# Moving every second q copy from VectorE to ScalarE, and re-ordering GpSimd's norms and first row gathers, in a spiking-attention and expert kernel

## What is computed

```python
Q, K, V = (lif(layer_norm(xn @ W.T + b), 1.0) for W, b in ...)       # spikes: 0 or 1
attn = Dh - (q_sum + k_sum - 2.0 * qk) + log_pe_bias(N, N)            # no softmax, so linear
out = lif(einsum(attn * scale, V), 0.5)
s = lif(layer_norm(out @ Wo.T + bo), 1.0)                             # output spikes
...
ids = argmin(dist2(rms_norm(xn), centroids))                          # one of 8 experts a row
y = einsum(a * silu(g), down_w[e])                                    # a, g = rms_norm(xn) @ up_w[e]
out = y + xn                                                          # of the row's own expert
```

## Time and profile before

| what | value |
|---|---|
| time, median of 3 runs | 383.24 us |
| lowest and highest | 380.7 and 385.92 us |
| the profiled execution's own time | 383.15 us |
| its span, from the first to the last instruction | 381.4 us |
| mean granted clock of PE | 0.991 of full speed |

### The profile page before, as it was taken

One profiled execution on the slowest core, in us unless ns is written; L12 is line 12 of the kernel. 1 busy time (PEld: TensorE's weight loads), 2 busy tenths in 40 slices (PEclk: granted clock), 3 DMA queues, 4 the chain that ended last, 5 costly groups with the idle time before them and its releaser, 6 DMA issues.

```text
span 381.4 us, 9230 instructions
## 1 busy us (share of the span) xinstructions
PE 359.4 (94%) x2455; PEld 302.9 (79%) x2464; DVE 310.2 (81%) x798; ACT 237.4 (62%) x631; POOL 239.4 (63%) x311
## 2 busy tenths in 40 slices
PE   8989999999998999997889999999999999999992
PEld 4768788877886888886778888888888888888881
DVE  5969999999978788998757777788877777788884
ACT  4477788878864768793535555555565555555561
POOL 4868577786760249986656666666666666666643
PEclk9999999999999999999989999999999999999998
DMA  7585668654359921565122222223223232232000
GB/s 222 185 273 183 162 195 227 225 146 140 111 129 218 238 83 57 167 188 152 51 84 79 66 71 87 69 80 96 77 81 84 79 89 76 90 95 63 29 16 0
DMA packets 31921, 45.42 MB, mean 119 GB/s; under 512 B 4161, under 2 KB 25858, under 8 KB 31764
## 3 DMA queue, kind: packets, MB, share of 16 engines
q1 hardware_dynamic: 25248, 29.73, 26.9%
q0 software_dynamic: 6416, 15.26, 14.0%
q10 hardware_dynamic: 228, 0.10, 0.1%
HBM read 36.84 MB, written 15.63 MB: 138 GB/s over the span
## 4 chain that ended last, share of the span: by engine, by line
PE 41%; DVE 27%; DMA 13%; issue 8%; ACT 5%; POOL 5%; DVEq 0%; ACTq 0%; POOLq 0%
PE bank L698 12%; PE bank L717 10%; DMA row_a<-rows_a,slot_id 9%; PE bank L501 3%; PE bank L615 3%; PE bank L576 3%; ACT d_hi L926 3%; DVE v_sp L1128 2%; DVE q_sp L1128 2%; DVE k_sp L1128 2%; PE bank L670 2%; PE bank L681 2%; DVE st L995 2%; DVE q_t L1139 2%; DMA thr<-lim_rows 2%
## 5 line engine op out<-in xcount | busy, mean ns | idle before, releaser
L1369 DVE TENSOR_TENSOR d_lo<-down_sb,d_hi 128x1024 fp32r<-128x1024 f32 x38 | 46.6, 1227 | 31.2 <-ACT d_hi L926 31.0
L1514 POOL DMA_INDIRECT row_a<-rows_a,slot_id x39 | 41.2, 1056 | 43.8 <-DVE e_o L1351 42.2
L926 ACT ACTIVATE d_hi<-down_sb 128x1024 fp32r x38 | 40.3, 1060 | 45.1 <-PE bank L717 35.4
L1562 POOL DMA_INDIRECT out_x<-e_o,slot_id x39 | 45.6, 1168 | 19.4 <-issue 14.1
L698 PE MATMUL bank<-up_hi,e_xh 128*128 x156 | 52.4, 417 | 0.0
L1520 POOL DMA_INDIRECT row_s<-rows_s,slot_id x39 | 39.1, 1002 | 15.9 <-issue 11.3
L698 PE MATMUL bank<-up_hi,e_xl 128*128 x156 | 48.5, 392 | 0.4 <-DVE e_xl L1310 0.4
L698 PE MATMUL bank<-up_lo,e_xh 128*128 x156 | 48.4, 392 | 0.0
L897 ACT ACTIVATE e_xh<-bank 128x256 fp32r<-128x256 f32 x39 | 15.0, 386 | 40.4 <-PE bank L670 40.4
L824 ACT ACTIVATE junk<-bank 128x256 bf16<-128x256 f32 x96 | 35.5, 380 | 6.7 <-PE bank L501 6.6
L501 PE MATMUL bank<-w_hi,x_hi 128*128 128x264 f32 (+1 forms) x128 | 35.6, 359 | 0.7 <-DVE dots L1132 0.7
(11 more groups left out here) (241 smaller groups left out, 981.3 us busy)
## 6 DMA issues: line engine op xcount, KB each, us to landing
up_raw<-in_up_w SPq DMA_DIRECT2D x16, 512.0 KB, 3.9
rows_a<-xn SPq DMA_DIRECT2D x32, 129.0 KB, 2.3
rows_a<-in_x SPq DMA_DIRECT2D x8, 512.0 KB, 11.8
xs<-in_x SPq DMA_DIRECT2D x7, 512.0 KB, 4.1
down_sb<-in_down_w SPq DMA_DIRECT2D x5, 512.0 KB, 6.1
rows_s<-s_out SPq DMA_DIRECT2D x8, 256.0 KB, 3.2
down_sb<-in_down_w SPq DMA_DIRECT2D x6, 256.0 KB, 3.1
blk_tab<-in_blocks SPq DMA_DIRECT2D x1, 1024.0 KB, 5.4
```

The costliest lines, as they stand in the source:

```text
L926: act.activation(d_hi[:, :, :], down_sb[:, bass.ds(e, 1), :, :].rearrange("p a c n -> p (a c) n"), ACT.Copy).then_inc(d_high, 1)
L1369: V.tensor_tensor(d_lo[:, :, :], down_sb[:, bass.ds(e, 1), :, :].rearrange("p a c n -> p (a c) n"), (d_hi if k < ST else d_end)[:, :, :].b ...
L1514: G.indirect_dma_start(row_a[s % 4][:, :], None, rows_a, bass.IndirectOffsetOnAxis(ap=slot_id[:, s:s + 1], axis=0), bounds_check=N - 1, oo ...
L1562: G.indirect_dma_start(out, bass.IndirectOffsetOnAxis(ap=slot_id[:, s:s + 1], axis=0), e_o[s % 4][:, :], None, bounds_check=N - 1, oob_is_ ...
```

## The change

Four things are changed.

1. In the projection stage the copy of the turned q tile of every odd tile but the last (tiles 1, 3, ..., 29: fifteen copies) is made by ACT, at the end of its step, instead of by DVE.
2. `norms_out` works on a whole chunk of four tiles: one addition and one power over four values a partition, where there were two of each over two values. It waits for all four squares, and DVE for all four factors.
3. POOL's first gathers stand in another order: after the norms of chunks 6 and 7 no gather is issued; `gather_a(2)` and `gather_a(3)` follow both; `gather_a(4)` comes after the first two `gather_s` instead of after the fourth.
4. In the last round of the attention ACT makes the squares of chunk 6 ahead of the last high part of the weights instead of behind it.

```diff
+        def kept_by_act(t):
+            return t % 2 == 1 and t < NT - 1
...
@@ (ACT, at the end of step_a)
+                if k >= 3 and kept_by_act(k - 3):
+
+                    act.wait_ge(qt_done, t - 2)
+                    act.activation(q_home(t - 3), qt_bank[:, 0:P].bitcast(BF16).rearrange("p (c n) -> p c n", c=DC),
+                                   ACT.Copy).then_inc(qt_kept, 1)
...
@@ (ACT, the attention's rounds)
                 attention_spikes(c)
+                squares_out((c - 1) % 2, (c - 1) // 2)
                 if c == NCH - 1:
                     high_parts(E - 1, (1,))
-                squares_out((c - 1) % 2, (c - 1) // 2)
...
@@ (DVE, at the end of step_a, and in output_spikes)
-                if 0 <= k - 3 < NT:
+                if 0 <= k - 3 < NT and not kept_by_act(k - 3):
                     keep_qt(k - 3, 0)
...
-                    dve.wait_ge(wo_rs, 2 * c + pair + 1)
+                    dve.wait_ge(wo_rs, c + 1)
...
@@ (POOL)
-                for pair in range(2):
-                    of = lambda buffer: buffer[:, bass.ds(c * CH + 2 * pair, 2), 3:4].rearrange("p a b -> p (a b)")
-                    held(wo_sq, CH * c + 2 * pair + 2)
...
+                of = lambda buffer: buffer[:, bass.ds(c * CH, CH), 3:4].rearrange("p a b -> p (a b)")
+                held(wo_sq, CH * (c + 1))
+                held(wo_rs, c - 1)
+                G.tensor_tensor(pv[:, k, :], of(ss), eps4[:, :], ALU.add).then_inc(out_n, 1)
+                held(out_n, c + 1)
+                G.tensor_tensor(of(rs), pv[:, k, :], half_neg[:, :, 0], ALU.pow).then_inc(wo_rs, 1)
...
-                if c >= 4 and c < NCH:
+                if c in (4, 5):
                     gather_a(c - 4)
+            gather_a(2)
+            gather_a(3)
             for k in range(2):
                 pool.wait_ge(s_put[k], 16 * NCH // 2)
-            for k in range(4):
-                gather_s(k)
+            gather_s(0)
+            gather_s(1)
+            gather_a(4)
+            gather_s(2)
+            gather_s(3)
...
             for s in range(4, ST):
-                gather_a(s)
+                if s > 4:
+                    gather_a(s)
                 gather_s(s)
                 scatter(s - 4)
```

More of the change, by code:

```diff
@@ L166, in build @@
         b16, _ = place("b16", [P, 24], BF16)
-        eps3, _ = place("eps3", [P, 3], F32)
+        eps4, _ = place("eps4", [P, CH], F32)
         half_neg, _ = place("half_neg", [P, 4, 2], F32)
@@ L307, in after, with q_home @@
                 eng.wait_ge(s, count)
+        def kept_by_act(t):
+            return t % 2 == 1 and t < NT - 1
+        def q_home(t):
+            c, at = t // CH, t % CH * P
+            return q_t[c // 2][:, c % 2, :, at:at + P]
         def x_tile(t):
@@ L1136, in keep_qt @@
                 dve.wait_ge(qt_done, t + 1)
-                at = k % CH * P
-                c = t // CH
-                V.tensor_copy(q_t[c // 2][:, c % 2, :, at:at + P],
+                V.tensor_copy(q_home(t),
                               qt_bank[:, 0:P].bitcast(BF16).rearrange("p (c n) -> p c n", c=DC)).then_inc(qt_kept, 1)
@@ L1402, in held @@
                 pool.sem_inc(pool_passed, 1)
-            G.memset(eps3[:, :], D * LN_EPS)
+            G.memset(eps4[:, :], D * LN_EPS)
             step(G.memset(half_neg[:, :, :], -0.5))
@@ L1434, in norms @@
                 held(rs_done, t - 1)
-                G.tensor_tensor(pv[:, s, 0:3], tile_of(ss, t)[:, 0:3], eps3[:, :], ALU.add).then_inc(norm_n, 1)
+                G.tensor_tensor(pv[:, s, 0:3], tile_of(ss, t)[:, 0:3], eps4[:, 0:3], ALU.add).then_inc(norm_n, 1)
                 held(norm_n, t + 1)
@@ L1501, in norms_out @@
                 c = k + 2 * i
-                for pair in range(2):
-                    of = lambda buffer: buffer[:, bass.ds(c * CH + 2 * pair, 2), 3:4].rearrange("p a b -> p (a b)")
-                    held(wo_sq, CH * c + 2 * pair + 2)
-                    held(wo_rs, 2 * c + pair - 1)
-                    G.tensor_tensor(pv[:, pair, 0:2], of(ss), eps3[:, 0:2], ALU.add).then_inc(out_n, 1)
-                    held(out_n, 2 * c + pair + 1)
-                    G.tensor_tensor(of(rs), pv[:, pair, 0:2], half_neg[:, 0, :], ALU.pow).then_inc(wo_rs, 1)
+                of = lambda buffer: buffer[:, bass.ds(c * CH, CH), 3:4].rearrange("p a b -> p (a b)")
[4 more added lines that the diff above has]
+                G.tensor_tensor(of(rs), pv[:, k, :], half_neg[:, :, 0], ALU.pow).then_inc(wo_rs, 1)
             def gather_a(s):
```

## The result

| | median us (range, runs) | ratio to before | 95% interval |
|---|---|---|---|
| the changed kernel | 380.62 (379.37 to 382.05, 15) | 0.9938 | 0.9911 to 0.9965 |
| the kernel before, beside it | 382.47 (380.70 to 386.02, 15) | 1 | |

The change makes the kernel 0.6% faster, where I had forecast 1.5%: 2.4 us by the ratio, 1.9 by the medians, against 5.7. The time lies inside the range (374.2 to 381.3), the gain is less than half of what I forecast. Two sizes have to be explained: what came, and what went away again.

A forecast was written before the change was run, and what follows sets the result against it. DVE's list was taken to bound the projections, then PE, with waits for rows in the expert steps. 383.15 - 3.6 (copies) - 2.0 (gathers, including the norms' 0.8) gave 377.5 us; range 374.2 to 381.3.

The forecast's parts named there:

- Part 1: Projections: eleven copies at 0.33 us leave DVE's chain, gaining 3.6 us, with PE late next.
- the bound of 5.0: Projections: upper limit of the copies' gain, all fifteen counting at 0.33 us, 5.0 us.
- rivals b and c: Projections: ACT becomes the bound; copies give nothing, 381.2 us, chance 0.10, or kernel slower than before, 387.2 us, chance 0.04.
- Part 2: Output norms before the experts: spikes end and first gather of spikes goes out 0.8 us earlier, bounds 0 and 1.0.
- the start of the spikes at 182.3: POOL's first gather of spikes, issued at 182.3 instead of 183.11 thanks to earlier norms.
- Part 3: First expert steps: reordered gathers start tile 5 at 197.0 instead of 198.97, gaining 2.0 us, bounds 1.1 and 4.0.
- The waits of 1 and 2.05 us: PE's waits for rows of tiles 4 and 5, forecast in place of one wait of 2.71 us.
- rival (a): First expert steps: tile 5's wait drops PE's clock, so the gather order gives 0.3, not 2.0; 379.2 us, chance 0.23.
- Part 4: Last attention round: squares of chunk 6 ahead of the high part gain nothing either way.

The follow-up runs named there:

- e10: Changed kernel with the old gather order and ACT copying q tiles 0 to 29 instead of every second one: 378.09 us, ratio 0.9870.
- e8: Kernel before with only the odd-tile copies on ACT and the norms by whole chunks: 375.58 us, ratio 0.9832.
- e1: Kernel before with only the odd-tile copies moved to ACT: 378.56 us, ratio 0.9938.
- e4: Changed kernel with the gathers back in their old order; copies, chunk norms and early squares kept: 375.08 us, ratio 0.9843.
- e5: The changed kernel measured and profiled once more, nothing altered, against the kernel before: ratio 0.9912.
- e3: Kernel before with the copies on ACT and the new gather order; norms in pairs and squares as before: 378.48 us, ratio 0.9930.
- e2: Changed kernel without the copies on ACT (DVE copies all q tiles): 383.07 us, ratio 1.0044.
- e7: Changed kernel with gathers for tiles 2 and 3 back between the norms, tile 4's kept early: 378.59 us, ratio 0.9920.
- e14: Changed kernel with eight expert steps written out before the loop instead of four: 379.93 us, ratio 0.9927.
- e6: Changed kernel with tile 4's gather back behind all four gathers of spikes, those for tiles 2 and 3 kept late: 377.26 us, ratio 0.9885.
- e11: Kernel of e6 with DVE's subtraction for `d_lo` cut into two halves: 380.52 us, ratio 0.9936.
- e9: Kernel before with only the norms by whole chunks: 384.48 us, ratio 1.0031.
- e12: Kernel of e9 with eight expert steps written out before the loop instead of four: 380.66 us, ratio 0.9948.
- e15: Kernel of e10 with eight expert steps written out before the loop instead of four: 375.46 us, ratio 0.9827.

## Why the prediction fell short

**Part 1, right in mechanism, too small: -4.5 where I had -3.6.** PE took over as I said, no engine waits for ACT's copies, and the bound of 5.0 holds. The term was mis-sized by the price of a copy. From the copy of tile 0 to that of tile 22 DVE now takes 61.8 us (26.99 to 88.78) instead of 66.6: 4.8 us for eleven copies, 0.43 each, which is the row's whole 0.415 and not the 0.33 that the chain puts on it. The chain's pieces overlap their neighbours; what leaves an in-order engine is the start-to-start distance. ACT never came near being the bound (rivals b and c): e10 gave it twice as many.

**Part 2, the step that failed first.** I booked 0.8 us for it, "inside" part 3. Beside the copies it is worth 4 us (e8 against e1: 0.9832 and 0.9938, 1.1%). In the table it turns tiles 0 to 5 from 32.3 into 28.0 us. Of these 4.3 us, 1.2 lie between tiles 0 and 2, where e1 has its wait of 2.04 us and the low clock. The other 3.1 are the wait for tile 4 (2.48 in e1, 2.71 before, 0.92 in e8) and the clock behind it. The reason is one that my own text had in hand: with the factors of the last chunk there earlier, the spikes land earlier (175.95 in e8, 178.29 in e1), and POOL has its four gathers out at 180.9, just as DVE ends tile 0 (180.93). From then on the fifth gather of rows waits for DVE and not for POOL's queue, and its issue, 1.94 us behind a `d_lo` in e1, takes 1.00. Only 0.9 us of the earlier landing are earlier spikes (the last write is issued at 172.8, not 173.7); the write itself took 3.1 us instead of 4.6, and what shortened it is not shown. I computed the start of the spikes at 182.3, 0.8 us earlier, and never asked what the *old* order would then do. I also did not see the price: POOL's one addition for four squares waits for the last of them, and stood 3.71 us behind DVE's `up_lo`. In all kernels with part 2 that costs PE a wait of 0.47 us in the last output projection and one of 1.04 instead of 0.39 in the first expert step, and is repaid.

**Part 3, the step that turned the gain: -2.0 forecast, +3.6 measured against e4 (+2.6 by e5's ratio).** The waits of 1 and 2.05 us came out as 0.85 and 2.05. The first error is in what they are compared with. I set them against the single wait of before, and credited part 3 with shrinking it. It does shrink it where the norms are in pairs (0.83 in e3, 2.48 in e1), but so does part 2 by itself (0.92 in e8), and the same wait can be taken away only once. The second error is in the new wait: also beside the old norms, where nothing else had shrunk the first one, part 3 gave 0.3 us by the ratios (e3 and e1) and not 2.0, since the wait for tile 5 was 2.75 us there, with the clock at 0.76 behind it. That is my rival (a), which had 0.3. Against e4 part 3 gives nothing at tile 4 and makes a wait of 2.05 to 2.78 us at tile 5 which otherwise doesn't exist. The mechanism is the one I described, "three other transfers have moved ahead of gather_a(5)", with a dead time of 2.14 us for POOL in front of them. The bounds for this part, 1.1 to 4.0 of gain, excluded a loss, and nothing that I gave as a reason excludes it.

**Rival (a)**, at 0.23, came true in e5, e2, e3, e7 and e14: waits of 2.70 to 2.78 us for tile 5, and a granted clock of 0.71 to 0.95 in the windows behind. In the first profile the wait was 2.05 and the clock stayed at 1.00. The 0.7 us between them are mostly an issue held by `d_lo`, which I had as a row, 1.70 us at 188.32, and took for the cost of a first issue. In the trace of before the `d_lo` of line 1369 runs from 187.93 to 189.16, and 188.32 + 1.70 lies 0.86 us behind its end. The Trainium skill (SBUF — State Buffer, on the two separate sides) states that GpSimd writes the descriptors of a DMA issued from its queue, for which it needs the port pair shared with DVE, and that DVE locks it out in a 2-port mode; of a DVE instruction with two inputs in SBUF it says that it holds the pair only against a GpSimd operation that reads SBUF. I cited that section for POOL's additions and not for its gathers. That `d_lo`, which has two inputs in SBUF, holds the issue of a gather is what e6 and e11 show, 1.93 us against 0.99; that the ports are the way in which it does is the page's account, and no run here tells it from another.

**Part 4** is nothing (e8 and e4), as said. **The base** was 383.15; beside the changed kernel the median of before was 382.47, and in the four later series 381.45 to 383.18. By ratio the forecast was 0.985; that e4 and e8, without part 3, have 0.984 and 0.983 is a coincidence of sums, since their gain is made of other terms.

**The gaps near the loop's entry** were in no part of the prediction. In the profile that has them tiles 5 to 8 take 3.7 us more than before. Whether something of the kind is hidden behind PE's wait of 2.71 us in the kernel before is not shown.

## What to carry to other kernels

When two edits meet in one wait, price each against a kernel that already has the other: both may take away the same wait, and the second one then only adds what it costs. Before a blocking wait is moved forward in an in-order queue, list what stands behind it and could have gone out in the idle time. And keep transfers that GpSimd issues out of the time in which DVE works on two SBUF operands, or cut that operation in pieces.

## What the runs showed of the hardware

- A gather that POOL begins to issue during DVE's 128x1024 subtraction of two SBUF operands ends 0.86 to 0.91 us after it (before, e5, e6): up to 1.93 us instead of 1.0. The exception is the one that began 0.03 us behind the subtraction (before, 183.11), which took 1.00. With the subtraction in two halves the issues up to 185 us took 0.99 to 1.16; later in e11 one gather took 1.28.
- In the expert steps 3 to 5, around the entry into a hardware loop at step 4, ACT and DVE stood still for 0.7 to 2.7 us at a time with no releaser in the kernel (changed, e9, e10, e11). With eight steps written out ahead of the loop such gaps are absent, at the old place and at the new one (e12 to e15). Two executions of one program differ in them (changed and e5).
- PE waits of 2.05 us (changed) and 2.12 (e3, at 171 us) left the clock at 1.00, one of 2.04 (e1, at 171 us) and all of 2.48 to 2.78 us were followed by windows with a mean between 0.66 and 0.95: near 2 us the length of the wait alone did not tell.
